# Attention steps whose outputs are issued behind the first unit's scores and turn, with cross slots in another order and the path bias elsewhere

## What is computed

```
x = layernorm(x + self_attention(x))             # 16 heads of 32, 4 key/value heads, causal
x = layernorm(x + cross_attention(x, ctx_512))   # 16 heads, keys and values from 128 features, causal
h = (cos(ph) + sin(ph)) * sigmoid(x @ amp_w + amp_b),  ph = pi * tanh(x @ ph_w + ph_b)
for l in 0, 1:
    h = layer_norm(h + (h @ ent_w[l] + ent_b[l]) @ ent_pw[l] + ent_pb[l]) * g3 + b3
    mod = cos(phase[l]) + sin(phase[l])
    h = layer_norm(h + sum_p (h @ path_w[l, p] + path_b[l, p]) * mod[p]) * g4 + b4
x = layernorm(x + h)
```

## Time and profile before

| | before |
|---|---|
| median of 3 runs | 1012.95 us (1012.87 to 1017.15) |
| profiled execution | 1010.36 us |
| its span, first to last instruction | 1008.6 us |
| mean granted TensorE clock | 0.961 |
| PE busy | 895.5 us (89%) |
| DVE busy | 682.7 us (68%) |
| ACT busy | 546.9 us (54%) |
| POOL busy | 494.4 us (49%) |

### The profile page before, as it was taken

How to read it: one execution, slowest core, us unless ns; L and a number is a source line. 1 busy time by engine, 2 the same in 40 slices (tenths; PEclk the granted TensorE clock), 3 DMA queues, 4 the chain that set the end, 5 groups by cost and what they waited for, 6 DMA issues and landing times. The chain is left out here.

```text
span 1008.6 us, 19361 instructions
## 1 busy us (share of the span) xinstructions
PE 895.5 (89%) x5892; PEld 744.3 (74%) x5892; DVE 682.7 (68%) x2055; ACT 546.9 (54%) x1674; POOL 494.4 (49%) x787
## 2 busy tenths in 40 slices
PE   4879998999778989999999999749899999999994
PEld 4778887888666778787787878537678778778773
DVE  4667777777685877786777767524757557567466
ACT  4555555555554565655655565616564564564461
POOL 0384544445274344644544442431466476476476
PEclk9889999999899999999999999869999999999998
DMA  4733434333755555475645425526000100100001
GB/s 130 215 126 121 148 125 140 135 114 140 249 159 176 159 179 158 138 222 174 199 127 186 132 97 174 161 80 263 13 1 32 54 1 32 53 1 32 10 1 42
DMA packets 79074, 118.52 MB, mean 118 GB/s; under 512 B 7920, under 2 KB 41744, under 8 KB 78224
## 3 DMA queue, kind: packets, MB, share of 16 engines
q1 hardware_dynamic: 78992, 117.52, 36.1%
HBM read 58.76 MB, written 17.83 MB: 76 GB/s over the span
## 5 line engine op out<-in xcount | busy, mean ns | idle before, releaser
L923 ACT ACTIVATE prob<-bank,nmax 128x128 f32<-128x128 f32 (+1 forms) x512 | 208.9, 434 | 102.5 <-DVE nmax L1035 102.5
L161 PE MATMUL bank<-w_ffn,hT 128*128 128x512 f32 x768 | 192.6, 402 | 0.0
L1035 DVE CUSTOM_DVE_ANT_0 bank<-bank,mask 128x128 f32<-128x128 f32 (+1 forms) x512 | 167.1, 382 | 7.5 <-PE bank L1211 5.4
L161 PEld LDWEIGHTS bank<-w_ffn,hT 128*128 128x128 f32 x768 | 141.4, 189 | 30.9
L161 PE MATMUL bank<-xT,w_att 128*128 128x256 f32 x864 | 125.6, 300 | 26.9 <-DVE w_att L947 10.6
L161 PEld LDWEIGHTS bank<-xT,w_att 128*128 128x128 f32 x864 | 117.0, 203 | 37.5 <-DVE xT L1023 9.7
L774 POOL TENSOR_TENSOR zone<-raw,zone 128x256 fp32r<-128x256 f32 x128 | 94.8, 775 | 66.4 <-ACT zone L894 66.4
L1223 PE MATMUL bank<-ident,prob 128*128 128x128 f32 x768 | 122.8, 285 | 3.5 <-ACT probT L910 3.5
L741 POOL TENSOR_SCALAR rwide<-rden 128x256 f32<-128x256 f32 x64 | 26.1, 408 | 194.7 <-DVE rden L1046 194.3
L923 ACT ACTIVATION_READ_ACCUMULATOR prob<-bank,nmax 128x1 f32 x512 | 112.1, 219 | 0.0
L1211 PE MATMUL bank<-k,q 96*128 96x128 f32 (+1 forms) x512 | 107.3, 314 | 2.2 <-DMA q<-stage 2.2
(11 more groups left out here) (119 smaller groups left out, 1554.9 us busy)
## 6 DMA issues: line engine op xcount, KB each, us to landing
q<-stage SPq DMA_DIRECT2D x192, 128.0 KB, 2.2
k<-kstage SPq DMA_DIRECT2D x48, 256.0 KB, 3.6
x<-xres SPq DMA_DIRECT2D x16, 512.0 KB, 3.5
raw<-in_ent_wT SPq DMA_DIRECT2D x32, 256.0 KB, 3.8
raw<-in_ent_pw SPq DMA_DIRECT2D x32, 256.0 KB, 4.2
raw<-in_xT SPq DMA_DIRECT2D x8, 512.0 KB, 3.5
raw<-in_path_w SPq DMA_DIRECT2D x8, 512.0 KB, 3.5
xres<-in_x SPq DMA_DIRECT2D x8, 512.0 KB, 5.0
```

What stands on the lines that cost most here:

```text
L161: ins = t.matmul(out, lhs(a, k), rhs(b, k), start=first and n == 0 and m == 0, stop=last and n == len(kts) - 1 and m == 2, skip_group_chec ...
L923: ins = s.activation(prob[:, u, c * width:(c + 1) * width], banks[u][:, c * width:(c + 1) * width], ACT.Exp, scale=-1.0, bias=nmax[:, i % ...
L1035: ins = v.tensor_tensor_reduce(scored, scored, mask[:, S - width:S], scale=-1.0, scalar=3e38, op0=ALU.add, op1=ALU.min, accum_out=nmax[:, ...
```

## The change

In a step, PE issues first the scores of unit A, then its turn, then the outputs of the group two steps back, and then scores and turn of B and of C, scores first. DVE does its output work behind the first maxima and the reciprocals. ACT copies a unit's turn behind the exponentials of the same unit, and unit A's copy waits for the outputs (`s_O`). In the cross slots, `cq 3` moves ahead of `cv 0`, and in the first cross turn `wo` moves to the ends of its steps. The path bias moves on POOL from the first turn to the steps 0 and 1 of the last self turn, cut in halves, and its store on SP from the start of that turn to behind its second step. The first turn's load of the next xT moves ahead on SP.

```diff
--- before.py
+++ after.py
@@ -249,16 +249,16 @@
         elif own == "cross" and after:
             out[0] += [U, U, ("cq", 2), U]
             if wo == "wo":
-                out[1] += [U, ("wo", 0), U, ("cv", 0), ("cq", 3), U, ("cv", 1), ("x1t", 0), ("x1t", 1)]
-                out[2] += [U, ("wo", 1), ("ck", 0), U, ("cq", 0)]
+                out[1] += [U, ("cq", 3), ("cv", 0), U, ("cv", 1), ("x1t", 0), ("x1t", 1), U, ("wo", 0)]
+                out[2] += [U, ("ck", 0), U, ("cq", 0), ("wo", 1)]
                 out[3] += [U, U, ("cq", 1), ("ck", 1)]
             else:
-                out[1] += [U, ("cv", 0), U, ("cq", 3), ("cv", 1), ("x1t", 0), ("x1t", 1)]
+                out[1] += [U, ("cq", 3), ("cv", 0), U, ("cv", 1), ("x1t", 0), ("x1t", 1)]
                 out[2] += [U, ("wout", 0), ("ck", 0), U, ("cq", 0)]
                 out[3] += [U, ("wout", 1), U, ("cq", 1), ("ck", 1)]
         elif own == "cross":
             out[0] += [("cq", 2)]
-            out[1] += [("cv", 0), ("cq", 3), ("cv", 1), ("gs", 0), ("gs", 1)]
+            out[1] += [("cq", 3), ("cv", 0), ("cv", 1), ("gs", 0), ("gs", 1)]
             out[2] += [("wout", 0), ("gs", 2), ("gs", 3)]
             out[3] += [("wout", 1), ("gs", 4), ("gs", 5)]
         else:
@@ -615,10 +615,10 @@
                 stack(pro, name)
 
             def body(t):
+                if t is first:
+                    wait_alone(q, s_xs, 1, s_passed)
+                    q.dma_start(xT_raw, xT_of[1]).then_inc(s_xT, 16)
                 if t is last_self:
-                    for l in range(NL):
-                        wait_alone(q, s_pbm, NL * NP + l + 1, s_passed)
-                        q.dma_start(A["fd"][l, 1][:, KT, :], acc[:, NP * l, :]).then_inc(s_pbst, 16)
                     load_piece(0)
                     q.dma_start(x1b[:, :, :], x1_of[0]).then_inc(s_x1, 16)
                 if t in (first_cross, crosses[0]):
@@ -634,7 +634,7 @@
 
                 def between(i):
 
-                    if i == 0 and t.after == "self":
+                    if i == 0 and t.after == "self" and t is not first:
                         wait_alone(q, s_xs, t.lin(1, 1), s_passed)
                         q.dma_start(xT_raw, xT_of[t.lin(1, 1)]).then_inc(s_xT, 16)
                     if i == 0 and t.before:
@@ -659,6 +659,9 @@
                         for n in range(1, 4):
                             load_piece(n)
                     if t is last_self and i == 1:
+                        for l in range(NL):
+                            wait_alone(q, s_pbm, 2 * l + 2, s_passed)
+                            q.dma_start(A["fd"][l, 1][:, KT, :], acc[:, NP * l, :]).then_inc(s_pbst, 16)
                         for n in range(4, PARKED):
                             load_piece(n)
                         wait_alone(q, s_xs, B, s_passed)
@@ -796,13 +799,16 @@
                         ins = g.tensor_tensor(pair[:, 0, c], pair[:, 0, c], pair[:, 1, c], ALU.add)
                     ins.then_inc(s_pc, 1)
 
-                def path_bias():
+                def path_bias(l):
                     g.wait_ge(s_pb, 16)
-                    for n in range(NL * NP):
-                        g.tensor_tensor(acc[:, n, :], acc[:, n, :], modb[:, n, :], ALU.mult).then_inc(s_pbm, 1)
-                    g.wait_ge(s_pbm, NL * NP)
-                    for l in range(NL):
-                        g.tensor_tensor(acc[:, NP * l, :], acc[:, NP * l, :], acc[:, NP * l + 1, :], ALU.add).then_inc(s_pbm, 1)
+                    for n in range(NP * l, NP * (l + 1)):
+                        for c in halves:
+                            ins = g.tensor_tensor(acc[:, n, c], acc[:, n, c], modb[:, n, c], ALU.mult)
+                    ins.then_inc(s_pbm, 1)
+                    g.wait_ge(s_pbm, 2 * l + 1)
+                    for c in halves:
+                        ins = g.tensor_tensor(acc[:, NP * l, c], acc[:, NP * l, c], acc[:, NP * l + 1, c], ALU.add)
+                    ins.then_inc(s_pbm, 1)
 
                 for i in range(t.steps()):
                     if t.turned(i):
@@ -811,8 +817,8 @@
                         split_output(i - 2)
                     if t.own == "self" and i == (2 if t is last_self else 3):
                         path()
-                    if t is first and i == 3:
-                        path_bias()
+                    if t is last_self and i < NL:
+                        path_bias(i)
                     for name in t.fillers(i):
                         if name[0] in ("wo", "wout"):
                             rstd_of(name)
@@ -904,18 +910,9 @@
 
             def body(t):
                 def step(i):
-                    if t.turned(i):
-                        s.wait_ge(s_T, t.groups(i - 2, U, 1))
-                        bank = banks[T_BANKS[(U * (i - 1)) % 2]]
-                        s.activation(probT[:, :, 0:P], bank[:, :].rearrange("p (j q) -> p j q", j=HG), ACT.Copy).then_inc(s_cp[0], 1)
-                    for u in range(U):
-                        if u and t.turned(i):
+                    def exponentials(u):
+                        if t.turned(i):
                             s.wait_ge(s_T, t.groups(i - 2, U, u + 1))
-                            if u in t.copied_by_scalar():
-                                bank = banks[T_BANKS[(U * (i - 1) + u) % 2]]
-                                s.activation(probT[:, 2 * (u - 1):2 * u, P:PW], bank[:, :].rearrange("p (j q) -> p j q", j=2), ACT.Copy).then_inc(s_cp[u], 1)
-                        if not t.scored(i):
-                            continue
                         s.wait_ge(s_max, t.groups(i - 1, U, u + 1))
                         heads = range(HG) if u == 0 else range(2 * (u - 1), 2 * u)
                         width, qt = (P, 0) if u == 0 else (S, 1)
@@ -923,6 +920,23 @@
                             ins = s.activation(prob[:, u, c * width:(c + 1) * width], banks[u][:, c * width:(c + 1) * width], ACT.Exp,
                                                scale=-1.0, bias=nmax[:, i % 2, qt, j:j + 1], accum_out=den[:, i % 2, qt, j:j + 1])
                         ins.then_inc(s_exp, 1)
+
+                    def copy(u):
+                        s.wait_ge(s_T, t.groups(i - 2, U, u + 1))
+                        bank = banks[T_BANKS[(U * (i - 1) + u) % 2]]
+                        if u == 0:
+                            if t.closed(i):
+                                s.wait_ge(s_O, t.groups(i - 2))
+                            out, src = probT[:, :, 0:P], bank[:, :].rearrange("p (j q) -> p j q", j=HG)
+                        else:
+                            out, src = probT[:, 2 * (u - 1):2 * u, P:PW], bank[:, :].rearrange("p (j q) -> p j q", j=2)
+                        s.activation(out, src, ACT.Copy).then_inc(s_cp[u], 1)
+
+                    for u in range(U):
+                        if t.scored(i):
+                            exponentials(u)
+                        if u in t.copied_by_scalar() and t.turned(i):
+                            copy(u)
 
                 for i in range(t.steps()):
                     step(i)
@@ -1056,13 +1070,13 @@
                     v.tensor_tensor(o32[:, i % 2, :], bank[:, 0:S], rT[:, i % 2, :], ALU.mult).then_inc(s_o, 1)
 
                 def step(i):
-                    if t.closed(i):
-                        output(i - 2)
                     for u in range(U):
                         if t.scored(i):
                             maxima(i, u)
                         if u == 0 and t.turned(i):
                             reciprocals(i - 1)
+                        if u == 0 and t.closed(i):
+                            output(i - 2)
                         if u not in t.copied_by_scalar() and t.turned(i):
                             probT_tile(i - 1, u)
 
@@ -1248,15 +1262,15 @@
                     ins.then_inc(s_O, 1)
 
                 for i in range(t.steps()):
-                    if t.closed(i):
-                        outputs(i - 2)
                     if t.scored(i):
                         kh, qh = stacked(i)
                     for u in range(U):
+                        if t.scored(i):
+                            scores(i, u, kh, qh)
                         if t.turned(i):
                             transposes(i - 1, u)
-                        if t.scored(i):
-                            scores(i, u, kh, qh)
+                        if u == 0 and t.closed(i):
+                            outputs(i - 2)
                     for name in t.fillers(i):
                         if t is last_self and name in (("ck", 0), ("cq", 0)):
                             t_.wait_ge(s_wlo, C_KEYS if name[0] == "ck" else C_QUERIES)
```

## The result

The changed kernel takes 1100.37 us (median of 4 runs, 1098.3 to 1103.27) against 1013.21 us of before in the same session; the ratio is 1.0853, 95% interval 1.0815 to 1.089. It is slower by 87 us. The forecast was 1075 us, so the sign held, and the new wait too, but the number lies at the very end of the range given (1036 to 1100), and a good quarter of the loss was not in the sum.

What follows compares the result with a forecast made beforehand. PE was taken to bound the attention turns, so its waits are paid for. 122.6 us of new waits less 59.6 us removed gave 63.0 us on top of 1010.4 or 1012.95, forecast 1075 us, range 1036 to 1100.

Steps and rivals of the forecast that it cites:

- the new wait: PE stands still before the turn of C until ACT has copied unit A's turn; 63 waits, 122.6 us added.
- The chain: Scores A, maxima, exponentials, copy, turn of C: 4.10 us even with engines free, against PE's arrival at 2.92 us.
- m: Time from a step's start until DVE's maxima start; 0.85 us at least, 1.0 to 3.7 in steps cited.
- the late rstd of POOL: First step of self turns: DVE's wait for POOL's rstd counted as hidden, making m 1.4 instead of about 3.5 us.
- The waits won back: PE waits removed for outputs, late items, ACT's copy, filler banks and smaller ones: 33.0 + 18.7 + 2 us.
- The clock: Half-clock time of the self turns, said to follow long waits before outputs, counted as 5.9 us gained.
- The clock falls more often: Rival: the new waits cause 16 more clock falls at about 1.55 us, 25 us more, 1100 us; chance 0.12.
- By turn: Attention turns lengthen: a self turn to near 35 us from 32.9, a cross turn to near 50 from 44.9.
- Slots, path bias, load of xT: Path bias costed at nothing in place; waits for rwide (2.8 us) and xT (2.1 us) removed; cross slots reduce filler waits.
- Replaced waits: Rival: DVE bounds a cross step, so the wait before C's turn only replaces others; 1036 us, chance 0.07.
- faster: Rival: the copy of A's turn is ready before PE reaches C's turn, chain under 2.92 us; 978 us, chance 0.05.
- no difference: Rival: the two sums meet by chance or C's turn waits less than read; near 1013 us, chance 0.04.

Runs made afterwards that it cites:

- e1: The changed kernel with ACT's copy of unit A's turn put back ahead of the exponentials of unit A: 992.69 us, ratio to before 0.9794.
- e3: The kernel before with only the new order within a step on PE, DVE and ACT; slots, path bias and xT load as before: 1098.87 us, ratio 1.0841.
- e5: The kernel before with only ACT's order changed, each copy behind the exponentials of the same unit; PE and DVE keep the old order: 1260.04 us, ratio 1.2444.
- e9: The changed kernel with five useless identity matmuls in front of each turn of C: 1083.24 us, ratio 1.0724.
- e2: The kernel before with only the reordered cross slots, moved path bias and earlier load of xT; old order within a step: 1012.15 us, ratio 0.9994.
- e4: The changed kernel with the turn of unit C issued on PE behind the step's first filler product instead of ahead of it: 1012.04 us, ratio 0.9989.
- e7: The 992.7 us kernel (copy of A first) with each unit's turn issued on PE ahead of its scores, outputs still behind unit A: 997.42 us, ratio 0.9825.
- the three versions at 992 us: The changed kernel with A's copy first (992.69 us), that plus C's turn behind the first filler (992.64), or all ACT copies before their exponentials (991.87).

## Why the prediction was right, and where it was short

- **The chain.** The forecast was m + 0.33 us in front of the turn of C, in 63 steps, 122.6 us: the rows show 63 waits of 116.2 us, and with the 0.18 us that each row hides 127.5 us. That it stands in the copy's place on ACT is shown by e1 (3.4 us left), e3 and e5. By step of a self turn: 1.73, 1.33, 1.33, 1.68 reckoned; 2.18, 1.03, 1.03, 1.56 in the rows, so about 2.36, 1.21, 1.21, 1.74 in delay. The first was too low: the text held the late rstd of POOL for hidden there, and DVE still waits for it (0.59 us at 167.91; its maxima start at 168.37, 2.1 us into the step, and not 1.4).
- **The waits won back**, 53.7 us without the clock: over the whole span PE's idle time grew by 61.4 us against 116.2 us of waits for the copy, so 54.8 us were won back, the 3.5 us of like waits before among them, as in the forecast. Right.
- **The clock** is the step that failed. The text took 5.9 us off, as the slow stretches behind the outputs' waits would go, and put "The clock falls more often" aside as a rival (0.12, 1100 us). That rival happened beside the forecast: PE's busy time grew by 31.5 us, 24 us of it by the clock, and e9 shows at least 17 us by the time. The text priced a fall at 1.55 us and spoke of 16 more; measured were 10 more at 2.4 us each, and the product is nearly the same. It listed 14 waits over 2.2 us and still left them out of its own sum. The cross turns of before, with their short waits at clock 1.00, were the wrong witness, as none of their waits was over 0.9 us. The section of "TensorE: Matmul & The Clock Gate" in the Trainium skill that was weighed there, "A second HAM failure mode: psum-queue depth-cycling", spoke for the rival; by that rule the trace of after agrees, with a mean clock of 0.93 in the attention part against 0.96, though here only the waits of 1.9 us and more were followed by a fall.
- **By turn.** A self turn was to take near 35 us instead of 32.9, a cross turn near 50 instead of 44.9. Read from one turn's first turn of C to that five turns later, they take 37.8 us (94.76 to 283.68) and 52.0 us (450.43 to 710.22). So both kinds of turn lie above the forecast, by 2.8 and 2.0 us; the self turns more, where the late rstd makes a wait of 2.2 to 2.4 us in each turn and the clock mostly fell behind it. The feed-forward part stayed at 331 us.
- **Restarts.** Behind a turn of C that has waited, the next filler starts after 0.41 us, without a wait 0.36 us (e1, 175.35 to 175.71); with the hidden 0.18 us a delay it makes some 14 us in the books of busy time, less what the waits of before had of the same. It was not in the sum.
- **Slots, path bias, load of xT.** Costed at nothing in place and a few us won back; e2 measures nothing (0.9974 to 1.0013). The fillers' waits were won back only together with the new step order, which makes PE late; by themselves the slots brought 13.0 us of waits for DVE.
- **Replaced waits, faster, no difference.** The first fell with e1 and e4: DVE was not the bound of a cross step. The faster case was right in its condition: with the copy ready before PE's 2.92 us the kernel is faster than before, 993 us in e1, not the 978 us given. Waits come back there (8.6 us for `xb`, where the earlier trace rows has 9.7, and 5.8 us of the outputs), and PE's idle time is 93.4 us against 113.1 before: 20 us less, where the rival had 35.

What is not settled: how the 7 us of busy time that the clock leaves split between hidden delay and restart; which of the parts of the new order on PE and DVE brings the gain of e1, beyond what e7 shows; and whether the three versions at 992 us differ at all.

## What to carry to other kernels

When work is moved ahead on one engine, follow each semaphore that the moved and the passed instructions count: here a copy that had been first in a queue went behind a chain over three engines, and the buffer that it frees is wanted a few matmuls later. Add up the chain by rows (0.85 + 1.13 + 1.39 + 0.73 us) and compare it with the time that the waiting engine takes to get there (2.92 us). And where a wait is new and comes in every step, price TensorE's clock with it: here it cost about a quarter of the new waits (24 of 113 us), and more than half of them where every wait was 2.7 us or longer (e5).

## What the runs showed of the hardware

- Useless matmuls in a wait can pay: five of the identity in front of each waiting turn raised the mean granted clock from 0.938 to 0.970 (2.4 GHz in all but 65 us of the span) and took 17 us off, with 39 us more busy time on PE.
- In the attention part of the changed kernel 20 of the 25 waits of PE of 1.9 us or more were followed by a stretch at 1.2 GHz, none of the 57 shorter ones. Each of the 10 stretches more than before cost about 2.4 us of PE's work.
- With 196.1 us of waits in 64 steps the mean clock was 0.874, and the same 5892 matmuls were busy for 1001.1 us instead of 895.5.
- The idle time in front of a matmul's row understates the delay by the overlap that the matmul would have had with the one ahead of it, 0.18 us here.
